# ScalarE's loads of the routed tiles: tiles 3 to 5 behind the last dense step, from tile 8 on one load a turn, four turns ahead

## What is computed

```python
x = x + tanh(g_xattn) * (0.6 * sigmoid(si + sj + b) + 0.4 * layernorm(x))   # 4 x 256 tokens of 256
xf = layernorm(x)                                      # 1024 tokens x 256
scores = sigmoid(xf @ w_router)                        # 32 experts
topk_idx = ...                                         # 6 experts per token, from the 4 best of 8 groups
routed = sum over the 6 chosen e of scores[e] * ((silu(xf @ gate_w[e]) * (xf @ up_w[e])) @ down_w[e])
shared = (silu(xf @ sh_gate_w) * (xf @ sh_up_w)) @ sh_down_w
out = x + tanh(g_ffn) * (routed + shared)
```

## Time and profile before

| | us |
|---|---|
| median of 3 runs | 249.18 (248.64 to 250.74) |
| the profiled execution's own time | 250.6 |
| its span, first to last instruction | 248.7 |
| PE busy in the span | 225.7 (91%) |
| ACT busy in the span | 78.2 (31%) |
| routed tiles, first transposes to the second dense expert | 84.9 to 222.2 |

### The profile page before, as it was taken

One profiled execution on the slowest core, in us unless ns is written; L12 is line 12 of the kernel. 1 busy time (PEld: TensorE's weight loads), 2 busy tenths in 40 slices (PEclk: granted clock), 3 DMA queues, 4 the chain that ended last, 5 costly groups with the idle time before them and its releaser, 6 DMA issues.

```text
span 248.7 us, 4830 instructions
## 1 busy us (share of the span) xinstructions
PE 225.7 (91%) x1051; PEld 175.0 (70%) x1052; DVE 130.5 (52%) x523; ACT 78.2 (31%) x220; POOL 137.1 (55%) x133
## 2 busy tenths in 40 slices
PE   7994998996899977988899999999999899999980
PEld 6893786884677754765677777777777678777760
DVE  2898588989744541333343434343434334442765
ACT  3635122110021121313435353444444344433220
POOL 6253747777777752344565657565656547565000
PEclk9778699999799996899999999999999999999996
DMA  6999999999999999799765658677666634447846
GB/s 203 279 284 304 407 372 346 319 359 329 337 374 344 367 227 327 164 269 227 141 110 116 112 103 154 111 130 105 114 108 121 104 36 59 55 55 116 259 138 225
DMA packets 39290, 51.67 MB, mean 208 GB/s; under 512 B 4942, under 2 KB 33710, under 8 KB 39270
## 3 DMA queue, kind: packets, MB, share of 16 engines
q1 hardware_dynamic: 24368, 29.81, 39.1%
q0 software_dynamic: 10416, 17.20, 34.1%
q10 hardware_dynamic: 4486, 4.44, 6.8%
HBM read 30.83 MB, written 20.61 MB: 207 GB/s over the span
## 4 chain that ended last, share of the span: by engine, by line
PE 67%; DVE 16%; DMA 5%; issue 4%; ACTq 3%; ACT 3%; POOL 1%; DVEq 1%
PE pG L765 21%; PE pY L779 15%; PE pG L704 5%; PE pX L759 4%; PE pH L773 4%; PE pG L864 4%; PE pG L788 4%; DMA xg<-rows_dram 3%; PE pY L715 3%; PE pY L807 2%; PE pY L884 2%; DVE xs L1267 2%; DMA wij<-in_L_xattn_W_dram 1%; ACTq L267 1%; ACTq L282 1%
## 5 line engine op out<-in xcount | busy, mean ns | idle before, releaser
L451 POOL DMA_INDIRECT sum_dram<-choice,idx x50 | 77.4, 1548 | 59.2 <-ACT choice L565 42.9
L765 PE MATMUL pG<-wgu,sdown 128*128 x200 | 69.8, 472 | 3.8 <-ACT sdown L553 2.8
L439 POOL DMA_INDIRECT rows_dram<-rows,row_i x48 | 47.0, 980 | 19.0 <-issue 14.1
L779 PE MATMUL pY<-wd,sup 88*128 x200 | 52.3, 384 | 0.0
L1193 DVE COPY sup<-pH 88x256 f32<-88x256 f32 x50 | 21.0, 420 | 55.1 <-PE pH L773 55.1
L765 PEld LDWEIGHTS pG<-wgu,sdown 128*128 128x128 f32 x200 | 35.1, 195 | 16.6 <-issue 6.2
L565 ACT ACTIVATE choice<-pY,wt 128x256 f32<-128x256 f32 x50 | 23.7, 473 | 55.3 <-PE pY L779 30.9
L779 PEld LDWEIGHTS pY<-wd,sup 88*128 88x128 f32 x200 | 34.6, 193 | 3.1
L773 PEld LDWEIGHTS pH<-ident,sgate 128*88 128x88 f32 x100 | 16.0, 161 | 12.5 <-issue 0.6
L558 ACT ACTIVATE sgate<-pG 128x176 f32<-128x176 f32 x50 | 15.9, 317 | 24.4 <-PE pG L765 23.6
L553 ACT ACTIVATE sdown<-pX 128x256 f32<-128x256 f32 x50 | 18.7, 376 | 7.9 <-PE pX L759 5.2
(11 more groups left out here) (188 smaller groups left out, 275.9 us busy)
## 6 DMA issues: line engine op xcount, KB each, us to landing
wgu<-in_L_ffn_gate_w_dram SPq DMA_DIRECT2D x8, 704.0 KB, 10.8
wgu<-in_L_ffn_up_w_dram SPq DMA_DIRECT2D x8, 704.0 KB, 11.4
wd<-in_L_ffn_down_w_dram SPq DMA_DIRECT2D x8, 640.0 KB
sum_dram<-zeros POOLq DMA_DIRECT2D x3, 1152.0 KB, 13.1
rows<-rows_dram ACTq DMA_DIRECT2D x18, 144.5 KB, 3.6
rows_dram<-zeros SPq DMA_DIRECT2D x8, 289.0 KB, 3.9
rows<-sum_dram SPq DMA_DIRECT2D x8, 256.0 KB, 3.8
xg<-rows_dram ACTq DMA_DIRECT2D x12, 144.5 KB, 2.8
```

The costliest lines, as they stand in the source:

```text
L439: pool.indirect_dma_start(rows_dram[:, :], bass.IndirectOffsetOnAxis(ap=row_i[:, j, k:k + 1], axis=0), rows[:, j, :], None).then_inc(done, 16)
L451: pool.indirect_dma_start(sums_dram[into[s]][:, :], bass.IndirectOffsetOnAxis(ap=idx[:, s:s + 1], axis=0), y[s % YRING], None, compute_op= ...
L765: ins = nc.tensor.matmul(pG[par][:, 0:2 * M].rearrange("t (g m) -> t g m", g=2), xT[:, par, k, :], wgu[:, bass.ds(e, 1), :, k, :].rearrang ...
L779: ins = nc.tensor.matmul(pY[par][:, 0:H], hT[0:MI, par, i, :], wd[:, bass.ds(e, 1), i, :], start=(i == 0), stop=(i == I - 1))
```

## The change

Tile 3 leaves the dense step 4; tiles 3, 4 and 5 are issued in a row behind the SiLU of the last dense step and ahead of the first two `copy_xT`; tile 6 takes the place behind them that tile 4 had. Tile 7 is issued in turn 0, and each tile t from 8 to 29 in turn t - 4, so that no turn has two loads. The loads themselves, their waits and SP's part are the same.

```diff
-    FETCH = {t: max((t - 5) // 2 if t < 2 * JH else (t - 1) // 2, t - XRING + 1) for t in range(5, HELD * ROUND)}
+    SURE = 3
+    SOONER = 7
+    FETCH = {t: t - SOONER if t < 2 * JH else t - JH for t in range(SOONER, HELD * ROUND)}
     SEGS = 3
...
                 silu_busy(j)
                 if j == 1:
                     act.wait_ge(s_scat, 16 * JH * TOPK)
-                if j <= JH:
+                if j <= SURE:
                     load(act, j - 1, j - 1)
+            for t in range(SURE, SOONER - 1):
+                load(act, t, t)
             copy_xT(0, 0)
             copy_xT(1, 1)
-            load(act, JH, JH)
+            load(act, SOONER - 1, SOONER - 1)
             silu(0, 0)
```

## The result

| | before | the change |
|---|---|---|
| median, us | 249.96 (248.64 to 252.61, 4 runs) | 262.31 (259.76 to 263.86, 4 runs) |
| the profiled execution's own time, its span | 250.6, 248.7 | 263.86, 262.0 |
| PE busy in the span | 225.7 (91%) | 230.5 (88%) |

The ratio is 1.053, 95% interval 1.045 to 1.061: slower by 5.3%, some 12 to 13 us, where 4.2 were forecast. The time lies outside the range of 248.5 to 258.5.

The account below looks back on a forecast made before the run. PE was taken to bound the kernel over most of the span. The terms -10.8 + 1.0 + 1.1 + 12.9 = +4.2 us, on the median 249.2, gave 253.4 us, slower, with range 248.5 to 258.5.

Parts of the forecast that it names:

- a fall of the clock: At the opening, two pauses of about 1 us bring PE's clock down: 2.8 us lost, 256.2 us; chance 0.08.
- the two old stretches: PE's longer stretches before, 89.05 to 103.29 and 108.29 to 124.85 us: 6.74 and 4.06 over plain turns, both go.
- opening, first gate and tile 3: Before the first turns: first gate product 1.0 us later behind three loads, tile 3's late load 1.1 more.
- tiles 8 to 13: Six turns while SP's zeros are in flight: 3.30 us each, 0.80 over plain, together 4.8.
- tiles 14 to 29: Sixteen later turns: 3.005 us each, 0.505 over plain, together 8.1.
- The law of the late turns: From tile 8 on, each load waits for a SiLU delayed by an earlier late tile; two turns take 3.60 + L, later 3.71 + L.
- L: Time from a load's issue to its landing: taken as 3.0 us for tiles 8 to 13, 2.3 for 14 to 29.
- a hidden look-up: PE's expert look-up stays hidden or half hidden at late loads; two turns 2.84 + L, 243.3 us, faster; chance 0.14.
- delays that come only in part: In the late turns, work in hand or short loads save 4.2 us: 249.2 us, no measurable change; chance 0.18.
- five more: Added to the high bound of 257.2 us if the loads beside the zeros took the pairs' 4.4 us.
- the rule of frequent short pauses: Skill rule: short pauses between matmul groups swing PE's clock; in later turns 2.8 us more each time.
- The quiet stretch: Turns of tiles 14 to 29, where loads landed after 2.2 to 3.0 us, median 2.2; 2.3 was taken.

Follow-up runs that it names:

- The opening alone: The changed kernel with tiles 3 to 6 as in the change, tile 7 in turn 0, loads from tile 8 on as before the change: 246.87 us, ratio 0.996.
- second profile of the change: The changed kernel run and profiled once more without an edit: 260.42 us, ratio 1.041.
- useless matmuls: The changed kernel with 20 matmuls, results never read, ahead of tile 8's transposes and 8 ahead of tile 10's: 261.5 us, ratio 1.046.
- loads alone: The kernel before, tiles 0 to 7 unchanged, each tile from 8 on issued four turns ahead as in the change: 264.67 us against 247.73 before.
- look-up first: The changed kernel with PE's look-up of the next tile's expert put ahead of the transposes and their wait for the load: 255.17 us.

## Why the prediction was wrong

The direction and the mechanism of the late turns were right, and the size was a third of what came: above all, one term was too small, and a fall of the clock came that had been given 0.08, and at another place. By the steps, in us on the path of PE:

| step | predicted | measured |
|---|---|---|
| the two old stretches go | -10.80 | -10.80 |
| opening, first gate and tile 3 | +2.1 | +3.37 |
| tiles 8 to 13 | +4.8 | +10.66 |
| tiles 14 to 29 | +8.1 | +9.75 |
| sum | +4.2 | +13.0 |

The measured column is worked out from the starts of the transposes, with the first row taken over as it was: 25.66 less 15.0 for tiles 8 to 13, 49.75 (128.07 to 177.82) less 40.0 for the next sixteen, and the opening as what is left of 6.74 when tile 6 is 3.37 ahead.

**What the change takes away** held. Tiles 4 to 7 follow each other at 2.50 (99.92 to 102.41 for the last), and no turn has two issues. The opening alone keeps 4.0 of it at tile 13, and its double loads cost the 4.1 that were read off.

**The law of the late turns** held: two turns are 3.60 + L. Its disputed part, the look-up behind the wait, was in the trace once, and the prediction weighed that one place against all the plain turns; moving the look-up confirmed it, and the rivals of a hidden look-up and of delays that come only in part fall. One turn more or less of lead did what the law says, but for the clock.

**The failed step is L beside the zeros: "so I take 3.0 for the six tiles 8 to 13".** Measured were 5.13, 5.0, 3.15, 4.1, 2.2 and 3.47, in the mean 3.84; by the law that is 2.5 of the 5.9 us by which these six turns came out dearer than forecast. The 3.0 rests on a misreading of the earlier trace rows, which took some loads for single and others for pairs. ACT's timeline before shows them (start us, us, what):

```profile
106.40 2.01 ACTq L282 DMA_DIRECT2D rows<-rows_dram  x2
...
116.69 1.91 ACTq L282 DMA_DIRECT2D xg<-rows_dram  x2
```

The load of 3.0, issued at 106.40, is the first of a pair (tiles 9 and 10, turn 4), and those of 2.7 and 2.9 are a pair too (tiles 15 and 16), behind the last issue of zeros; the one single load of the stretch, at 103.69, has no landing in that trace. So these rows could not tell singles from pairs, and tiles 8 and 9 came singly and took 5. With the zeros held back the six loads took 2.2 to 3.6, and the next two, beside the zeros, 4.8 and 4.2, which shows who lengthens them. By how much, the place does not settle: issued 0.1 us ahead of the first zeros, tile 8's load took 4.61 in the second profile of the change (101.69, zeros from 101.78) and 2.98 with the useless matmuls (100.91, zeros from 101.02). What sets the two apart stays open. The prediction's price for L at the pairs' 4.4, "five more", is 4.2 by its own law, or 257.6.

**The rest is in the main the clock's**, as far as the rows go. By the law the measured loads, 3.84 in the mean, give six turns of (3.60 + 3.84) / 2, or 22.3; the stretch took 25.66, 3.3 more. A second count: the turns from tile 8 to 9 and from 10 to 11 ended with the load long there (105.0 + 5.0 and 115.3 + 4.1 are before 112.69 and 121.84), so PE's own work set them; they took 4.84 and 5.45, where such a turn at full clock took 3.35 later (140.80 to 144.15): 1.5 + 2.1 = 3.6. Some 0.5 of either count is the longer look-up at tile 10 (0.87 us): the gate products came 1.52 behind the transposes there and not 0.99. That leaves 2.8 and 3.1. The two counts come near each other, but they are worked out and not shown apart: the kernels in which the clock held in this stretch (20.89 with one transfer of zeros, 23.06 with the useless matmuls, 19.39 without zeros) all changed L or PE's work too. The prediction had this rival at the opening, with 0.08 and 2.8 us, and looked for a clock of 1.00 from 85 to 160; it was 0.57 from 108 to 112, behind a wait of 2.78 where an L of 3.0 would have made one of 0.8. Waits of 0.84 left the clock at 1.00 (tile 15 here, tile 10 with the loads one turn earlier), so the second miss probably follows from the first; no run shows it. In the later turns, with a short pause in every second turn, the clock stayed at 1.00 (128 to 160): the rule of frequent short pauses that the prediction weighed is not borne out there.

**The opening** was short by 1.3. The first issue came 1.37 after the SiLU began (82.86 to 84.23), not 0.93, so the first gate came 1.66 later and not 1.0; tile 3's load took 7.33, where the rows of before had 6.4 to 7.1, and its late gate was paid in full.

**The quiet stretch** was short by 1.7. Most loads took 2.2, as in the earlier trace rows; those in the chain of waits took 2.61 and 3.35. Two turns were 5.86 to 6.11, near the 6.0 forecast, except up to tiles 15, 19 and 29 (6.87, 6.43 and 6.71). A median over all loads is too low for the ones that count. What makes some of them longer was not tried. The Trainium skill, DMA: Bandwidth & Descriptors, section "Anatomy of one DMA — SWDGE (gpsimd) path", puts a transfer's time at a constant and its bytes, fitted on GpSimd's path; that is 2.34 us by estimate here. Most loads of the quiet stretch agree (2.2), the 5.0 and 5.13 of the same bytes beside the zeros do not.

## What to carry to other kernels

When a load is issued behind work that itself waits for an earlier load, write down the round trip (landing to next issue, plus L) and set it against the lead in turns: below it every turn pays, for good, and one turn more of lead ends it. Take L from the loads that will be in the same company, and from the longest of them, not from the ones that look most like yours in form, and look up for each row how it was issued; near the edge the price of a wrong L is paid in each turn, and a wait of some us can cost the clock on top. What stands behind a wait on a sequencer, such as the load of a register, is hidden only while the engine still has work in hand when the wait ends: put it ahead of the wait.

## What was not expected of the hardware

A 144.5 KB load took 2.2 us in the quiet stretch, 5.0 to 5.13 beside the first of the 289 KB zero transfers (2.98 in another run), and 7.33 beside the weights: more than a factor of three at the same size and queue. And a wait of a given length does not settle the clock. Gate products took 2.71 after waits of 2.57, 2.78 (the change), 2.75 (loads alone) and 2.30 (zeros held back), but 1.40 after 2.72 with the look-up first, where the row by stretch says a clock of 1.00 throughout:

```profile
108.00:112.00 4.00, 1.66 (x8) 0.97 (x7) 1.00 (x4) 0.94 (x3) 2.10 (x2) 1.00 1.07 235
```

Shorter waits differ too: 1.35 was followed by 1.45, and 1.39 by 2.71, in one run (zeros held back), 1.32 by 2.52 in another (loads alone). What tells these apart stays open.
